# Six of sixteen sequences routed beside the blocks of an expert stage, with TensorE's router step between two products

## What is computed

```
x = x + 0.5 * moe0(layernorm(x))      # silu(h w1) * (h w3), then w2; hidden 256      ffn 0
x = x + attn0(layernorm(x))           # 16 heads of 8, window of 32 keys
x = x + 0.5 * moe0(layernorm(x))      # the same weights again                        ffn 1
x = x + 0.5 * moe1(layernorm(x))      # gelu(h W1 + b1) W2 + b2; hidden 512           ffn 2
z = layernorm(x); x = x + z + attn1(layernorm(z) * ln_w + ln_b)   # 16 heads of 8, all keys
x = x + 0.5 * moe1(layernorm(x))      # the second layer's weights again              ffn 3
```

## Time and profile before

| | us |
|---|---|
| median of 3 runs | 3025.9 (3025.2 to 3033.7) |
| span of the profiled execution | 3022.4 |
| TensorE busy | 2350.3 (78%) |
| VectorE busy | 2147.5 (71%) |
| ScalarE busy | 1635.4 (54%) |
| GpSimd busy | 1531.1 (51%) |

### The profile page before, as it was taken

The page is one execution under the profiler, slowest core; times in us unless marked ns, Lnnn a source line. Parts: engine busy times, 40 slices in busy tenths (PEclk is TensorE's granted clock), DMA queues, the critical chain, the costliest instruction groups (busy, mean ns, idle before and its releaser), DMA issues.

```text
span 3022.4 us, 74232 instructions
## 1 busy us (share of the span) xinstructions
PE 2350.3 (78%) x24646; PEld 1530.8 (51%) x24646; DVE 2147.5 (71%) x6077; ACT 1635.4 (54%) x3371; POOL 1531.1 (51%) x1644
## 2 busy tenths in 40 slices
PE   2328958999999588532699489999999999958990
PEld 1217746777777477422588323333333333327880
DVE  3636657778776467686577488888888888846775
ACT  1116634555555366311577247777767667747770
POOL 4770034666653477577100555566565653145871
PEclk9999978999999799755799679999999999979995
DMA  8123323223322244332322111111111111012226
GB/s 171 43 64 104 104 68 88 81 79 80 84 79 59 57 116 119 98 96 71 90 87 84 60 47 40 39 49 52 40 47 47 47 37 44 19 33 77 86 85 177
DMA packets 250053, 222.84 MB, mean 74 GB/s; under 512 B 67078, under 2 KB 230668, under 8 KB 249164
## 3 DMA queue, kind: packets, MB, share of 16 engines
q1 hardware_dynamic: 216028, 148.82, 17.9%
q0 software_dynamic: 33664, 69.27, 7.6%
HBM read 114.00 MB, written 107.53 MB: 73 GB/s over the span
## 4 chain that ended last, share of the span: by engine, by line
PE 53%; POOL 14%; DVE 8%; issue 8%; ACT 4%; DMA 4%; SPq 1%; POOLq 0%; DVEq 0%; ACTq 0%
PE PS L525 10%; POOL choice_outputs L1116 8%; PE PS L705 8%; PE PS L529 6%; PE PS L674 6%; PE PS L653 6%; PE PS L616 5%; POOL slot_inputs L1107 4%; DVE xr L1268 3%; PE PS L723 2%; ACT arena L854 2%; PE PS L657 2%; PE PS L661 2%; DVE mxs L1494 2%; PE PS L682 1%
## 5 line engine op out<-in xcount | busy, mean ns | idle before, releaser
L964 ACT ACTIVATE arena<-PS 128x512 f32<-128x512 f32 (+1 forms) x1344 | 699.1, 586 | 284.7 <-PE PS L674 163.2
L1494 DVE TENSOR_REDUCE mxs<-PS 128x1 f16<-128x512 f32 x1024 | 650.6, 685 | 113.3 <-PE PS L653 103.4
L1107 POOL DMA_INDIRECT slot_inputs<-xs,slots x512 | 510.4, 997 | 414.1 <-PE PS L674 211.2
L1173 POOL DMA_INDIRECT G<-block_outputs,places x256 | 253.8, 991 | 654.7 <-DMA block_outputs<-arena 424.2
L653 PE MATMUL PS<-w,q 96*128 96x512 f16 x1024 | 398.8, 391 | 31.7 <-DVE mxs L1494 30.1
L674 PE MATMUL PS<-q,w 100*128 100x512 f16 x1024 | 390.6, 384 | 18.4 <-ACT arena L964 18.3
L1116 POOL DMA_INDIRECT choice_outputs<-arena x284 | 325.8, 1147 | 131.3 <-issue 83.0
L854 ACT ACTIVATE arena<-PS 128x256 f16<-128x256 f32 (+2 forms) x586 | 257.6, 440 | 225.4 <-PE PS L529 165.3
L529 PE MATMUL PS<-ident,arena 128*128 128x128 f32 x1084 | 204.1, 290 | 157.3 <-DMA arena<-slot_inputs 107.9
L1498 DVE TENSOR_REDUCE mxs<-PS 128x2 f16<-128x320 f32 x512 | 243.0, 492 | 117.3 <-PE PS L661 112.4
L1432 DVE TENSOR_TENSOR arena<-PS,arena 128x256 f16<-128x256 f32 x284 | 120.4, 424 | 238.0 <-ACT arena L854 238.0
(11 more groups left out here) (192 smaller groups left out, 4277.5 us busy)
## 6 DMA issues: line engine op xcount, KB each, us to landing
arena<-slot_inputs SPq DMA_DIRECT2D x284, 129.0 KB
block_outputs<-arena SPq DMA_DIRECT2D x142, 128.0 KB, 1.7
qk_parts<-qk SPq DMA_DIRECT2D x64, 256.0 KB, 2.4
G<-choice_outputs SPq DMA_DIRECT2D x64, 256.0 KB
q<-qk_parts SPq DMA_DIRECT2D x128, 96.0 KB
slot_inputs<-xs,slots POOLq DMA_INDIRECT x512, 2.4
qk_parts<-qk SPq DMA_DIRECT2D x64, 128.0 KB, 2.5
W<-qk_parts SPq DMA_DIRECT2D x128, 48.0 KB
```

The lines of the kernel that those rows point to most:

```text
L964: activate(pT[:, u % PTR, 0:n], PS[:, SC0 + u % NSC[a], 0:n], ACT.Exp, scale=SCALE).then_inc(s_pe, 1)
L1107: g.indirect_dma_start(Xs, bass.IndirectOffsetOnAxis(ap=slots[:, s, c, k:k + 1], axis=0), xs[:, n % XSR, c if f % 2 else 0, k], None).then ...
L1173: g.indirect_dma_start(G[:, s % 2, k, c], None, Ys, bass.IndirectOffsetOnAxis(ap=places[:, s, c, k:k + 1], axis=0))\
L1494: vec.tensor_reduce(mxs[:, m % 2, p % NT, QROWS + col:QROWS + col + 1], PS[:, MX0 + u % NMX], AX, ALU.max)\
```

## The change

Ten sequences (JOIN) are routed in the router stage. The counts after the ninth (EARLY) give 29 full blocks (FULL) that can be listed then: full_blocks makes that list, and SP loads these blocks once the scatters of the ninth sequence have landed. The other six sequences are routed in the block loop of ffn 0 and ffn 2: sequence 10 + i takes the iterations 1 + 3 i to 7 + 3 i, and in step k of its seven each engine does a part, named in beside_block of that engine. GpSimd runs beside_ffn, its own order of powers and scatters. With sequence 15 VectorE lists the other 42 blocks (other_blocks), and SP writes the padding and waits for the rest ahead of block 29. TensorE does its part between up(b) and down(b - 2). The transposes of blocks have one PSUM bank (6) in ffn 0 and 2, since bank 7 (RB) is the router's. rows_in_blocks works in four parts, at iterations 37, 45, 53 and 61. In ffn 2, SP's fetches of sequences 12 to 15 for the combine stand among its block loads. In the second layer's routers, ffn 3's in attention 1 too, ScalarE takes Tanh of half the argument in place of Exp, and VectorE makes the exponential of it with three more instructions on 128 x 36. ffn 1 and ffn 3 have one list, as before. ScalarE's kz copies come three iterations earlier. The scratch of the lists lies in q3 in place of the arena.

```diff
+EARLY = 9
+APART = 3
-UB, YB, XB = 0, 4, 6
+UB, YB, XB, RB = 0, 4, 6, 7
...
+    FULL = EARLY * T * 2 // BS - (E - 1)
+    JOIN = EARLY + 1
...
+        def listed(f):
+            return (s_tab, f // 2 + 1) if f % 2 == 0 else (s_rest, f + 1)
+
+        def xbanks(f):
+            return 1 + f % 2
+
+        def beside(f, b):
+            if f % 2:
+                return []
+            return [(s, b - 1 - APART * (s - JOIN)) for s in range(JOIN, SEQS) if 0 <= b - 1 - APART * (s - JOIN) <= 6]
...
+            def rows_scattered(f, s):
+                for c in range(2):
+                    for k in range(XSR):
+                        sp.wait_ge(s_scat[c][k], scattered(f * SEQS + s, k))
+
+            def rest_listed(f):
+                sp.wait_ge(s_cnt, f + 1)
                 for e in range(E):
                     first = sp.value_load(padi[0:1, e:e + 1], min_val=0, max_val=E * CAP - BS)
                     sp.dma_start(Xs[bass.ds(first, BS)], Pad[e * BS:(e + 1) * BS]).then_inc(s_pad, 16)
-                sp.wait_ge(s_tab, 2 * f + 2)
-                for c in range(2):
-                    for k in range(XSR):
-                        sp.wait_ge(s_scat[c][k], scattered((f + 1) * SEQS - 1, k))
+                sp.wait_ge(s_rest, f + 1)
+                rows_scattered(f, LASTS)
                 sp.wait_ge(s_pad, (1 + (f + 1) * E) * 16)
 
+            def ffn(f):
+                if f % 2 == 0:
+                    sp.wait_ge(*listed(f))
+                    rows_scattered(f, EARLY - 1)
+                else:
+                    rest_listed(f)
                 for b in range(NBLK + STLAG):
+                    if f == 2 and b < NBLK:
+                        for s in range(JOIN + 2, SEQS):
+                            if b == APART * (s - 2 - JOIN) + XRING + 3:
+                                fetch(1, s)
+                    if f % 2 == 0 and b == FULL:
+                        rest_listed(f)
...
             def between(f):
-                for s in range(SEQS):
+                for s in range(JOIN + 2):
...
-                for i in range(SEQS + 1):
+                for i in range(JOIN + 1):
...
                 def turned(b):
                     pe.wait_ge(s_xld[b % XRING], 16 * (f * -(-(NBLK - b % XRING) // XRING) + b // XRING + 1))
-                    if b >= 2:
-                        pe.wait_ge(s_xev, blk(f, b - 2))
+                    if b >= xbanks(f):
+                        pe.wait_ge(s_xev, blk(f, b - xbanks(f)))
                     for j in range(BJ):
-                        ins = turn(PS[:, XB + b % 2], xb[:, b % XRING, j, 0:D], P, ident[:], j * P)
+                        ins = turn(PS[:, XB + b % xbanks(f)], xb[:, b % XRING, j, 0:D], P, ident[:], j * P)
...
+                def beside_block(b):
+                    for s, k in beside(f, b):
+                        if k == 2:
+                            if s > JOIN:
+                                pe.wait_ge(s_rpr, nth(f, s - 1))
+                            router_in(f, s, RB)
+                        if k == 3:
+                            router_logits(f, s, RB)
+                        if k == 4:
+                            pe.wait_ge(s_rlr, nth(f, s))
+                            router_positions(f, s, RB)
+
                 expert(0)
                 expert(1)
                 turned(0)
@@ -628,6 +684,9 @@
                         turned(b + 1)
                     if b < NBLK:
                         up(b)
+                    beside_block(b)
+                    if f % 2 == 0 and b == LAG:
+                        pe.wait_ge(s_rpr, nth(f, JOIN - 1))
                     if b >= LAG:
                         down(b - LAG)
...
             def router_exp(f, s):
                 eng.wait_ge(s_rdl, nth(f, s))
-                if f < 2:
-                    activate(ex[:, 0:NT], dl[:, 0:NT], ACT.Tanh, scale=0.5).then_inc(s_rex, 1)
-                else:
-                    activate(ex[:], dl[:], ACT.Exp).then_inc(s_rex, 1)
+                n = NT if f < 2 else NT * E + NT
...
-                    if i >= 8 and i - 8 < KR and f % 2 == 0:
+                    if i >= 5 and i - 5 < KR:
...
+                def beside_block(b):
+                    for s, k in beside(f, b):
+                        if k == 3:
+                            router_inT(f, s, RB)
+                        if k == 5:
+                            router_exp(f, s)
...
+            def beside_ffn(f):
+                router_rstd(f, JOIN)
+                for s in range(JOIN, SEQS):
+                    scatter(f, s, 0, range(NT))
+                    if valid(s + 1):
+                        router_rstd(f, s + 1)
+                    scatter(f, s, 1, range(NT))
...
+                link(vec.tensor_scalar(dl[:], ex[:], -1.0, 1.0, ALU.mult, ALU.add))
+                link(vec.reciprocal(dl[:], dl[:]))
+                link(vec.scalar_tensor_tensor(ex[:], ex[:], 1.0, dl[:], ALU.add, ALU.mult))
...
+            def full_blocks(f):
+                vec.memset(tdone[:], 0.0)
+                link(vec.memset(tshift[:], 0.0))
+                counted(f, EARLY - 1)
+                link(vec.tensor_tensor(tcmp[:], bcast(tcnt[:], 32), kstep[:, :, 1:33], ALU.is_ge))
+                link(vec.tensor_reduce(tnb[:], tcmp[:], AX, ALU.add))
...
+                list_blocks(f, 0, FULL)
+                v.sem_inc(s_tab, 1)
...
+            def other_blocks(f):
+                first = FULL if f % 2 == 0 else 0
                 counts = posr[0:1, (f * SEQS + LASTS) % 2, NT]
-                F = HID[f] * P
-                vec.tensor_copy(padi[:], counts).then_inc(s_tab, 1)
-                link(vec.tensor_tensor(tcnt[:], posr[:, (f * SEQS + LASTS) % 2, NT], ebase[:], ALU.subtract))
-                link(vec.tensor_tensor(tcmp[:], bcast(tcnt[:], 32), kstep[:], ALU.is_gt))
...
+                n = NBLK - first
+                blocks_of(n, E - 1)
+                if first:
+                    link(vec.tensor_scalar(tbase[:], tdone[0:1, 0:1], float(BS), None, ALU.mult))
+                    link(vec.tensor_scalar(toff[:, 0:n], toff[:, 0:n], tbase[:], None, ALU.add))
+                list_blocks(f, first, n)
+                v.sem_inc(s_rest, 1)
...
+            def rows_in_blocks(f, i):
+                at = slots[:, 4 * i:4 * i + 4].rearrange("p s c k -> p (s c k)")
+                n = 8 * NT
+                link(vec.tensor_tensor(past, bcast(at, 2 * E), bcast(tfrom[:].rearrange("p e i -> p (e i)"), n, 1), ALU.is_ge))
+                link(vec.tensor_tensor(past, past, bcast(tjump[:], n, 1), ALU.mult))
                 link(vec.tensor_reduce(back[:], past, AX, ALU.add))
-                vec.tensor_tensor(places[:].rearrange("p s c k -> p (s c k)"), at, back[:], ALU.subtract).then_inc(s_plc, 1)
+                ins = vec.tensor_tensor(places[:, 4 * i:4 * i + 4].rearrange("p s c k -> p (s c k)"), at, back[:], ALU.add)
+                if i == SEQS // 4 - 1:
+                    ins.then_inc(s_plc, 1)
...
+                    if i == EARLY:
+                        full_blocks(f)
...
+                def beside_block(b):
+                    for s, k in beside(f, b):
+                        if k == 0:
+                            if f:
+                                combine(f - 1, s)
+                                v.wait_ge(s_cmb, nth(f - 1, s))
+                            elif s % (SEQS // 4) == 0 or s == JOIN:
+                                v.wait_ge(s_xin[s // (SEQS // 4)], 16 * SEQS // 4)
+                            router_stats(f, s)
+                        if k == 2:
+                            router_norm(f, s)
+                        if k == 4:
+                            router_top(f, s, RB)
+                            router_places(f, s)
+                            router_diff(f, s)
+                        if k == 5:
+                            router_slots(f, s, RB)
+                        if k == 6:
+                            router_weights(f, s)
+                            if s == LASTS:
+                                other_blocks(f)
+
...
+                    beside_block(b)
+                    if f % 2 == 0 and b > FULL and (b - FULL) % 8 == 0 and (b - FULL) // 8 <= SEQS // 4:
+                        rows_in_blocks(f, (b - FULL) // 8 - 1)
```

More of the change, by code:

```diff
@@ L868, in router_exp @@
                 eng.wait_ge(s_rdl, nth(f, s))
-                if f < 2:
-                    activate(ex[:, 0:NT], dl[:, 0:NT], ACT.Tanh, scale=0.5).then_inc(s_rex, 1)
-                else:
-                    activate(ex[:], dl[:], ACT.Exp).then_inc(s_rex, 1)
+                n = NT if f < 2 else NT * E + NT
+                activate(ex[:, 0:n], dl[:, 0:n], ACT.Tanh, scale=0.5).then_inc(s_rex, 1)
             def routers(f):
-                for i in range(SEQS + 1):
+                for i in range(JOIN + 1):
                     if valid(i - 1):
                         router_exp(f, i - 1)
-                    if valid(i):
+                    if i < JOIN:
```

(39 more changed lines are left out.)

108 lines of the change are left out of this document (64 added, 44 removed).

## The result

| | us |
|---|---|
| median of the changed kernel, 4 runs | 3076.1 (3074.4 to 3080.5) |
| median of the kernel before beside it, 4 runs | 3029.8 (3025.2 to 3034.7) |
| ratio, with 95% interval | 1.0154 (1.0137 to 1.0172) |
| span of the profiled execution | 3072.7 (before 3022.4; 50.3 more) |

The changed kernel is 1.5% slower: 46 us by the medians. The forecast was 18.6 us slower, 3044 us. The direction and the range held, the size did not.

A forecast was written before the change was run, and what follows sets the result against it. TensorE was taken to bound the ffn 0 and ffn 2 loops, GpSimd the router stages. -159.6 + 149.4 + 11.6 + 11.2 + 4 + 2 = +18.6 us gave 3044 us, range 2990 to 3085.

The forecast's parts named there:

- What bounds the kernel: TensorE sets the pace of the ffn 0 and ffn 2 loops; GpSimd's scatters and power set the two router stages.
- The start: Both router stages: first block seven periods earlier, 78.2 and 79.0 us, plus one power less; together 159.6 us gained.
- The wait: ffn 0 and ffn 2, five times each: VectorE's norm waits 6.06 us for GpSimd's four scatters and a power.
- The cycles: Three blocks beside routing take 21 us in ffn 0 and 26 in ffn 2, costing 149.4 us together.
- The walk with half rate for 5 us: Engine queues walked with TensorE's clock halved for the first 5 us: cycles of 21.2 us in ffn 0, 26.9 in ffn 2.
- Sequence 10 and the second list: Sequence 10 costs 4.6 us in ffn 0, 7 in ffn 2; VectorE's other_blocks list costs 4.6 and 6.6.
- The attention: Attention 1: 16 x 0.6 us more on VectorE, busy 83%, costs 0 to 10 us; 2 taken.
- ScalarE's tables: Tanh among Silu and Gelu may need table loads, up to 2 x 1.28 us a sequence; 0 to 5 us, 0 taken.
- Single bank, block 29, SP's queue: ffn 0 and ffn 2: one transpose bank, block 29's later load and SP's added fetches cost nothing; 5 us if block 29's margin goes.
- Rival (2): Cycles sit on VectorE's floor, 17.1 + 22.6 = 39.7 us, under the 43.3 break-even: 2997 us, faster; chance 0.20.
- Rival (3): Clock stays low for 9 us in either loop, cycles 23.6 and 28, block 29 late: 3070 us; chance 0.21.
- Rival (4): Power ready before the norm, so VectorE doesn't wait: cycles near 11.5 and 17.5, 90 us less, 2954 us; chance 0.05.

The follow-up runs named there:

- the run with the exponential ahead of the blocks: Kernel with power ahead of scatters, fourth-router exponential and TensorE's step behind the second product, plus Exp for the third router's ten early sequences: 2951.5 us, ratio 0.9759.
- the run with six: Kernel before with six added VectorE instructions for the fourth router, its exponential kept: 3054.0 us, ratio 1.0102.
- the run with the power first: Changed kernel with GpSimd issuing the next sequence's power ahead of both groups of scatters, not between them: 2988.7 us, ratio 0.9887.

## Why the prediction was right or wrong

**What bounds the kernel.** Right, and the run with the exponential ahead of the blocks shows it for the third router stage: it belongs to GpSimd's scatters.

**The start.** The first block reaches TensorE at 154.89, 74.2 us earlier, for 79.4 forecast; in the third stage 78.1 for 80.2. Of the first shortfall 2 us lie before the sixth power of the stage (77.18, before 75.12). In the nine other kernels with the changed first router stage the first block came at 150.7 to 152.2 us, in the five with the old one at 227.5 to 229.1: some 76.5 us by their medians, so part of the shortfall is how one execution went, and some 3 us of it stay. Together 7.3 us too much.

**The wait.** Right in place, number and cause: the earlier trace rows gave 6.06 us, the trace 6.32, five times in each loop; TensorE's hole was put at 7.6 and is 6.6 to 7.8. Taking it away gave 81 us, doubling it cost 50.

**The cycles.** 20.5 for 21, and 27.4 four times and 22.5 once for 26: 5 x 20.5 - 5 x 7.75 = 63.8 and 131.9 - 5 x 9.38 = 85.0, together 148.8 us for 149.4. The walk with half rate for 5 us, nearest which the forecast was put, has its row: after the hole that ends at 186.28 the granted clock is 0.50 up to 190 and 1.00 from 192 on (rows in the last section). In ffn 2 the walk undercounted the second hole, before the one-hot, after which the clock is low again (behind the holes that end at 1409.08 and 1436.27 the granted clock is 0.50 from 1411 to 1413 and from 1437 to 1439): 1.4 us too few in each of the four; that the fifth has no combine of a next sequence in it made up for most of them, and the 0.5 us too many in each cycle of ffn 0 for the rest. That the sum came out within 0.6 us is in part luck.

**Sequence 10 and the second list.** In ffn 2 the first six blocks lost 11.9 us for 7 forecast, and what follows block 21 (the list and rows_in_blocks) 13.8 for 9.6. Combine and statistics stand ahead of three blocks' evacuations in VectorE's queue, and the listing makes one block last 11.9 us for 3.1. Both are above the price and within the bounds; together 9.1 us. In ffn 0 the like came to 2.8 us.

**The attention: the step that failed.** "16 x 0.6 us more on VectorE, which is busy 83% there ...: 0 to 10, I take 2." The stage became 19.4 us longer, which the forecast itself had named as a sign of being wrong. Three errors lie in the one term. The instructions are 0.85 us, not 0.6, from the start of the first to the start of what follows them (the changed kernel's timeline, VectorE):
```profile
2338.63 0.17 DVE L1421 TENSOR_SCALAR dl<-ex 128x36 f32<-128x36 f32 x1
2338.84 0.38 DVE L1422 RECIPROCAL dl<-dl 128x36 f32<-128x36 f32 x1
2339.25 0.20 DVE L1423 SCALAR_TENSOR_TENSOR ex<-ex,dl 128x36 f32<-128x36 f32 x1
2339.48 0.19 DVE L1424 TENSOR_REDUCE zsum<-ex 128x4 f32<-128x32 f32 x1
```
The busy share of 83% was read as room, where the order of VectorE's queue leaves none at this place: 16 x 0.85 = 13.6 us are paid whole, and the second set of three again (16 us). And 0 to 10 left out the clock: with the three instructions more sequences run at a granted clock of 0.97 or 0.94 (windows beside the run with six), and that is some 1 to 8 us by the runs with three instructions (15 and 22 us, less 13.6). Why the clock falls in one sequence and not in the next is not shown; that TensorE's holes, longer by what VectorE does, bring the falls is the author's estimate, which no run tested. The whole account, in us over the forecast: 17.4 here, 7.3 at the starts, 9.1 and 2.8 in the loops beside the waits, -0.6 in the waits, -4.5 in attention 0 and ffn 1: 18.6 + 31.5 = 50.1 of the 50.3.

Those 4.5 us stay open. They lie in ffn 1: from the last statistics of attention 0 to the first of the third router stage the kernel before, the one with one bank and the one with Tanh alone take 246.3 to 248.4 us (the two with instructions added 247.7 and 248.6), and the ten with the change's early start 240.9 to 245.1. So the gain comes with the change, but no run was made for its cause.

**ScalarE's tables.** Right at zero: the profile after lists seven table loads of 1.28 us and the one before eight; none stands beside Tanh, which runs 64 times. The upper bound, two loads a sequence, is not borne out by this trace.

**Single bank, block 29, SP's queue.** Right at zero: the bank by its own run, the other two by the absence of any hole at block 29 (the products of blocks 28 to 31 follow one another in 2.5 to 2.7 us in ffn 0 and in 3.1 to 3.2 in ffn 2).

**The rivals.** Rival (2) put the cycles on VectorE's floor, 39.7 us for the pair, and said that the pair decides at 43.3 us. With the last cycle of ffn 2 taken into the mean, 26.4, the changed kernel had 46.9, not on that floor, and was slower; with the power first it had 31.1 (12.6 and 18.5) and was faster. That the pair decides held; the point was placed too high. With all other terms as measured, 50.3 - 148.8 = -98.5 us, it lies at 17.1 + 98.5 / 5 = 36.8 us. Rival (3) named 3070 us, nearer the measured time than the forecast, but from cycles of 23.6 and 28 and a late block 29; the cycles were shorter than both and block 29 was not late, so its number came close by luck. Rival (4), the power ready before the norm, is what the run with the power first made: it gave cycles of 11.5 and 17.5 and 90 us less, the run 12.6, 18.5 and 81.

## What to carry to other kernels

When a step is interleaved into a loop, the order inside the queue of the engine that seems to have time to spare can decide: a small instruction that another engine waits for goes ahead of long issues that nobody waits for yet (81 us here). Price each instruction added to a chain at its start-to-start distance and at full value, unless its place in the timeline shows idle time right behind it; a stage's busy share of 83% is no such proof. And put a step that others wait for ahead of the own work, but behind work that is ready, on each engine separately: TensorE gained 22 to 29 us by doing its ready product first, VectorE lost 54 us by doing its own work first.

## What the runs showed of the hardware

In the mixed stretches the waits went with a clock that falls: the ten waits are 63 us, taking them away gave 81, and the granted clock of the two stretches rose from 0.75 and 0.74 to 0.94 and 0.84. Windows of 2 us of the changed kernel, over one cycle of ffn 0, columns as in the earlier trace rows:
```profile
184.00:186.00 2.00, 0.00 (x0) 0.00 (x0) 1.06 (x5) 0.00 (x0) 1.80 (x2) 0.50 0.10 33
...
188.00:190.00 2.00, 2.00 (x15) 1.63 (x13) 0.48 (x3) 0.90 (x3) 1.70 (x2) 0.50 0.20 66
190.00:192.00 2.00, 2.00 (x16) 1.66 (x15) 1.90 (x12) 1.01 (x3) 0.10 (x1) 0.72 0.10 33
192.00:194.00 2.00, 2.00 (x27) 1.88 (x27) 1.20 (x4) 1.17 (x4) 0.00 (x0) 1.00 0.19 66
194.00:196.00 2.00, 0.62 (x12) 0.35 (x10) 1.86 (x18) 0.96 (x3) 0.00 (x0) 1.00 0.26 66
...
198.00:200.00 2.00, 1.99 (x10) 1.05 (x8) 0.98 (x4) 0.74 (x3) 0.51 (x1) 0.50 0.07 22
```
The granted clock is 0.50 when TensorE wakes from the hole at 186.28, 1.00 from 192 on, some 5 us later, and 0.50 again from 198 on, while TensorE is busy and the next hole has not begun; ahead of that fall it was busy for 0.62 us from 194 to 196.

Tanh ran beside Silu and Gelu without a table load of its own: the changed kernel's seven loads stand at the first instruction of the program (0.80 us), at the first Silu of ffn 0 and ffn 1 (157.8 and 1049.7), at the first Exp of each attention (475.9 and 1790.5) and at the first Gelu of ffn 2 and ffn 3 (1383.6 and 2780.7), 1.28 us each, and none with the 64 Tanh. A reciprocal over 128x36 took 0.38 us, where a scalar operation on the same tile took 0.17 (medians of 32 each in the changed kernel, 378 and 173 ns).
